# Eight destinations per packed adjacency column, with two-bit counts from destination 256 on

## The chip, the core and the metric

The kernel runs on one core of one Trainium2 chip. The metric is device time in microseconds (us), the median of several runs. TensorE (PE in the profile) multiplies, VectorE (DVE), ScalarE (ACT) and GpSimd (POOL) work on elements, SyncE (SP) issues DMAs.

## The reference

A graph of 6250 nodes and 200000 edges, sorted by destination, goes through two SAGE layers and three message-passing layers. Each of the five needs the sum over all edges into a node of the features of the edge's source:

```python
agg = segment_sum(x[src], dst, num_segments=n)          # SAGE, twice: mean @ W_l.T + b_l + x @ W_r.T
m = concatenate([x[dst_f], x[src_f], ea_f], axis=1) @ W.T + b
agg = segment_sum(m, dst_f, num_segments=n)             # three times, with relu and a batch norm between
```

Destinations are drawn as `6250 * uniform ** 2`, so low node numbers have many edges and high ones few. Sources are uniform.

## The kernel before, in words

The kernel first builds the dense matrix of edge counts (source by destination, as 8-bit floats) and then multiplies node features with it five times.

**The build (function build).** Destinations are cut into windows, and each window into slots of at most 128 edges. There are NS = 1983 slots. For a slot, TensorE multiplies two tables that VectorE makes from the digits of the edges' sources and destinations: `lo` (128 source digits) and `key` (destination lane and source block). One matmul adds the counts of a few *packed columns* to a PSUM bank. A packed column holds four destinations: each has a 4-bit lane of one 16-bit number. A bank holds 8 packed columns of 52 numbers, so 32 destinations, and there are 196 banks, in a ring of RING = 4 PSUM buffers.

The work goes in *half-steps* h of HS = 64 slots (NH = 31 of them), and each engine's order is written out in the code:

- VectorE in half-step h: `large(h)` (one table `lo`, L786, and some pieces of `key`, L793), `attributes(c)` for one chunk c of the edge attributes (L820 to L828), at even h `small` (digit tables for 128 slots, L751 to L770), at odd h `digits` (L736 to L747), then `unpack(f)` for the stages that have become whole. `large(h)` waits until TensorE is through with the slots of half-step h - 2 (`s_pe`).
- ScalarE in half-step h: `high(c)` (L982), `take(f)` (L1017), `evacuate(g)` of the banks that TensorE ended in half-step h - 1 (L998, one bank each, into 16-bit numbers in F), `sums` (L1008), `low(c)` (L988), at even h `across` (L973, L974), which waits for `small`, and `natural` (L959).
- TensorE in half-step h: `product(f)` (L904, 49 matmuls) for the stages that were unpacked after half-step h - 1, then the 64 slots (L929), then chunk c (L942).

A *stage* is 256 destinations, one of NST = 25. `unpack(f)` (L810, L811) takes the packed numbers of the f-th stage apart into 8-bit floats, GpSimd stores them (`keep`), and TensorE multiplies them at once with the first layer's features: `product(f)` for f < 21 (EARLIER), `remaining(f)` (L314) for the last four. All `product`s share one PSUM buffer PX, so the second of two in one half-step waits until ScalarE has taken the first:

```python
def product(f):
    pe.wait_ge(s_un, f + 1)
    if f >= 1:
        pe.wait_ge(s_raw, f)          # take(f - 1) on ScalarE
```

ScalarE does `take(f)` one half-step later in its own order (`for f in multiplied_after(h - 2)`).

`unpack(f)` writes to one of two buffers, so it waits until the stage before the last has been multiplied: `s_px` for `product`, `s_fin` for `remaining`:

```python
v.wait_ge(*((s_px, f - 1) if f - 2 < EARLIER else (m["s_fin"], f - 1 - EARLIER)))
```

**The end of the build.** After the last chunk VectorE makes reciprocals of the early edge counts (`counts`, L1092 to L1098). SyncE then stores them (L587), reads them back over all partitions (`reciprocals`, L299), reads the stored products (L292), the transposed input x (`given`, L305) into F, and the late edge counts (L600). When these are there VectorE does `counts` again and unpacks the last stage, and all engines meet at the end of the block.

**The layers (function propagate).** Five passes of 13 blocks of 512 destinations. In pass 0 the products are already there. In passes 1 to 4 TensorE multiplies 49 x 512 columns per block (L1462). VectorE's `sums` (L1834, L1836) bring the columns, which stand lane by lane in the stored matrix, into their natural order. VectorE's `check` (L1866) adds up the stored matrix in seven rounds, ScalarE's `lanes` (L1995) adds up each lane, and at the end these are compared with the edge counts, so that an overflow of a lane would be seen and a slow general version (`restart`, `general`) run instead.

Of the kernel before, what the change touches and what calls it, by code (L numbers as in the profile page):

```python
# [7 lines left out]
E = 200000  # L8
NT = 49
# [21 lines left out]

def bands(a, b):
# [4 lines left out]
    for j in range(ns):  # L37
        met = [i for i in range(b - a) if most(mu[i + 1]) > 128 * j and mu[i] - Z * math.sqrt(mu[i]) < 128 * (j + 1)]
        if j == 0:
            met.append(0)  # L40
        if j == ns - 1:
            met.append(b - a - 1)
        found.append(((a + min(met)) // 4, (a + max(met)) // 4 - (a + min(met)) // 4 + 1))
# [3 lines left out]
def cut(a, b):  # L47

    best = {b: (0.0, [])}
    for x in range(b - 4, a - 4, -4):  # L50
        options = []
        for y in range(x + 4, b + 1, 4):
            w = bands(x, y)
            if max(q for _, q in w) <= 4:
# [20 lines left out]
BANK = 32  # L75
BANKS = [cut(a, a + BANK) for a in range(0, NP, BANK)]
# [37 lines left out]
SLOT = [(x // 4, j, qa, width, i == 0, i == len(w) - 1)  # L114
# [5 lines left out]
NBK = NP // BANK  # L120
RING = 4
LAST_OF = [max(k for k in range(NS) if SLOT[k][2] // 8 == b) for b in TURN]
BEGUN = {st: min(g for g in range(NBK) if TURN[g] // 8 == st) for st in range(NST)}
DONE = {st: max(g for g in range(NBK) if TURN[g] // 8 == st) for st in range(NST)}
STAGES = sorted(range(NST), key=lambda st: DONE[st])
RANK = {st: f for f, st in enumerate(STAGES)}
HOME, BEFORE = {}, {}
for _st in sorted(range(NST), key=lambda st: BEGUN[st]):
    _users = {h: max((DONE[x] for x in HOME if HOME[x] == h), default=-1) for h in range(4)}
    HOME[_st] = min(_users, key=lambda h: _users[h])  # L130
    assert _users[HOME[_st]] < BEGUN[_st]
    BEFORE[_st] = max((RANK[x] + 1 for x in HOME if HOME[x] == HOME[_st] and x != _st), default=0)
# [103 lines left out]
GIVEN = [(0, 2), (2, NB)]  # L236
# [3 lines left out]
def stage_width(s):  # L240
    return SW if s < NST - 1 else LASTW

# [28 lines left out]
def spread(m, name, cnt, a, b):  # L271

    x = (m["ea_sum"][32, :] if name == "ea_sum" else m[name])[a:b]
    return x.rearrange("(p c) -> p c", p=16), cnt[:, 0:(b - a) // 16]
# [49 lines left out]
def gnn(nc, ins, out):  # L324
    ctx = ExitStack()
    with ctx:
# [3 lines left out]
        def sem(name):  # L330
# [32 lines left out]
            "csum": sb("csum", [16, 2, 4]),  # L363
# [13 lines left out]
def build(nc, ins, m):  # L377
    ctx = ExitStack()
    with ctx:
# [28 lines left out]
        nb = within(0, [128, TS], f32)  # L408
# [41 lines left out]
        packed = m["F"][:].bitcast(u16).rearrange("p (r c) -> p r c", r=4)  # L450
# [92 lines left out]
        def _(sp):  # L543
# [3 lines left out]
            sp.dma_start(nb[:], ins["c_nb"]).then_inc(s_con, 16)  # L547
# [20 lines left out]
            for c in range(NCH):  # L568
# [6 lines left out]
                if c == NCH - 2:  # L575
                    for i in range(2):
                        sp.wait_ge(s_eo[i], 16 * (EARLY // SW // 2))
                    there, here = spread(m, "ea_sum", cnt, 0, EARLY)
                    sp.dma_start(here, there).then_inc(m["s_cl"], 16)
# [11 lines left out]
            sp.wait_ge(m["s_cd"], 16)  # L591
# [11 lines left out]
            sp.wait_ge(m["s_cr"], 8)  # L603
# [3 lines left out]
            given(sp, ins, m, 1)  # L607
# [90 lines left out]
        def _(v):  # L698
# [30 lines left out]
            def digits(t):  # L729
# [9 lines left out]
                op(d[:, 3], node, -4, None, ALU.bitwise_and)  # L739
                op(d[:, 4], node, 4, 0x20, ALU.logical_shift_left, ALU.bitwise_and)  # L740
                op(d[:, 5], node, 6, 0x40, ALU.logical_shift_left, ALU.bitwise_and)
# [57 lines left out]
            def unpack(f):  # L799
# [1380 lines left out]
```

## Time and profile before

| what | value |
|---|---|
| runs of the kernel before | 1074.97, 1079.38, 1078.5 us, median 1078.5 us |
| the profiled execution's own time | 1073.11 us |
| its span, first to last instruction | 1071.3 us |
| busy in the span: PE, DVE, ACT, POOL | 923.9, 686.6, 406.3, 131.8 us |
| mean granted TensorE clock | 0.951 of full speed |
| end of the build, where all engines meet | 405 us after the span's start |

The busy times are those of the whole span, and an engine's share differs much between the build (up to 405 us) and the layers (after it). A time in the trace is counted from the span's start. Where instructions of VectorE follow each other without a wait, each begins a little before the one ahead has ended, so the step from start to start is what one costs.

### The profile page before, as it was taken

The page shows a single profiled execution, that of the slowest core. Times are in us where ns is not written, and L with a number is a line of the kernel's source. Part 1 is how long each engine was busy: PE and PEld are TensorE (multiplying, and loading weights), DVE is VectorE, ACT ScalarE, POOL GpSimd, SP SyncE. Part 2 cuts the span into 40 slices and gives each one's busy share as a digit, 9 for nine tenths or more (in the row PEclk, how much of TensorE's full clock was granted, in tenths as well). Part 3 has the DMA queues.
Part 4 walks back from the last instruction along what each step waited for, and adds up shares of the span by engine and source line. Part 5 has one row for each costly group of instructions (what it writes and reads, how often), then busy time and mean ns, then how long its engine had stood idle before and what let it go on. Part 6 is the DMA issues. An engine that isn't in the chain of part 4 may idle for free. (4 is left out here: it accounts for less than half of the span.)

```text
span 1071.3 us, 19165 instructions
## 1 busy us (share of the span) xinstructions
PE 923.9 (86%) x7566; PEld 566.3 (53%) x7566; DVE 686.6 (64%) x1288; ACT 406.3 (38%) x847; POOL 131.8 (12%) x150
## 2 busy tenths in 40 slices
PE   0357877979788778999999999997999997999995
PEld 0356776878687765545555544444444444444443
DVE  6898989999999954624433756655395456332334
ACT  2684788888888821100000010104411022401113
POOL 4212313244232320000000000000000000000001
PEclk9868989889899998999999999998999998999998
DMA  6735546756665497964774607776018775037771
GB/s 145 182 97 183 190 137 196 254 160 197 197 207 173 125 338 234 364 247 150 306 312 184 251 22 301 305 266 258 16 33 324 290 281 242 10 115 289 270 282 31
DMA packets 65160, 218.63 MB, mean 204 GB/s; under 512 B 28986, under 2 KB 42891, under 8 KB 51523
## 3 DMA queue, kind: packets, MB, share of 16 engines
q1 hardware_dynamic: 55444, 164.26, 43.2%
q0 software_dynamic: 9616, 53.04, 14.5%
q8 instruction: 62, 1.02, 0.4%
q14 instruction: 38, 0.31, 0.1%
HBM read 170.43 MB, written 45.22 MB: 201 GB/s over the span
## 5 line engine op out<-in xcount | busy, mean ns | idle before, releaser
L1462 PE MATMUL PM<-Aring,Xop 128*128 128x512 fp8e4 (+1 forms) x1960 | 396.7, 363 | 2.3 <-issue 2.3
L1462 PEld LDWEIGHTS PM<-Aring,Xop 128*128 128x128 f16 x1960 | 182.3, 98 | 214.1 <-issue 11.3
L1462 PE MATMUL PM<-Ares,Xop 128*128 128x512 fp8e4 x588 | 136.4, 387 | 2.7 <-ACT Xop L2074 1.2
L1836 DVE TENSOR_SCALAR S<-PM 128x256 f32<-128x256 f32 x72 | 30.6, 424 | 153.2 <-PE PM L1462 64.8
L929 PE MATMUL PM<-Aring 128*128 128x104 fp8e4 (+3 forms) x1616 | 95.2, 217 | 35.1 <-ACT F L998 35.0
L2025 ACT ACTIVATE F<-PH,bag 64x512 f32<-64x512 f32 (+1 forms) x39 | 25.7, 659 | 260.8 <-PE PH L1679 260.3
L929 PEld LDWEIGHTS PM<-Aring 128*128 128x128 fp8e4 x1616 | 85.7, 103 | 38.1 <-ACT F L998 36.9
L1462 PEld LDWEIGHTS PM<-Ares,Xop 128*128 128x128 f16 x588 | 56.0, 99 | 70.1 <-issue 7.3
L1592 POOL DMA_DIRECT2D out<-hT x12 | 9.0, 754 | 652.1 <-DVE hT L1793 652.1
L786 DVE TENSOR_TENSOR Aring<-Ares 128x4096 uint16<-128x4096 uint16 x31 | 70.9, 2287 | 4.9 <-PE PW L929 4.6
L998 ACT ACTIVATE F<-PM 128x392 uint16<-128x392 f32 x147 | 66.6, 516 | 6.7 <-PE PM L929 5.4
L1866 DVE TENSOR_TENSOR hT<-hT,Aring 128x1536 uint16<-128x1536 uint16 (+2 forms) x71 | 67.6, 952 | 2.3
L793 DVE TENSOR_TENSOR Aring<-Ares 128x1144 uint16<-128x1144 uint16 (+22 forms) x139 | 67.4, 551 | 0.0
L904 PE MATMUL PX<-Aring,Xop 128*128 128x256 fp8e4 x490 | 57.0, 278 | 6.9 <-ACT Ares L1017 6.9
L904 PE MATMUL PX<-Xop 128*128 128x256 fp8e4 (+1 forms) x539 | 59.5, 272 | 0.6 <-ACT Ares L1017 0.6
L1834 DVE TENSOR_TENSOR S<-PM,rc 128x256 f32<-128x256 f32 (+1 forms) x25 | 9.4, 415 | 76.5 <-PE PM L1462 74.2
L929 PE MATMUL PW<-Aring 128*128 128x104 fp8e4 (+3 forms) x535 | 34.5, 210 | 26.3 <-ACT F L998 24.2
L904 PEld LDWEIGHTS PX<-Aring,Xop 128*128 128x128 f16 x490 | 48.4, 100 | 13.3 <-issue 7.0
L904 PEld LDWEIGHTS PX<-Xop 128*128 128x128 f16 x539 | 51.3, 100 | 7.1 <-issue 0.8
L2017 ACT ACTIVATE st_<-st_ 128x4 f32<-128x4 f32 (+1 forms) x13 | 2.7, 205 | 131.6 <-DVE st_ L1767 131.6
L942 PE MATMUL PA<-Ares,ea 128*128 128x64 f16 (+1 forms) x1000 | 42.0, 208 | 3.5 <-ACT odd L1009 3.5
L882 PE MATMUL PT<-ident,Ares 128*128 128x128 f32 x32 | 8.7, 365 | 39.9 <-ACT Ares L960 39.9
(170 smaller groups left out, 1265.6 us busy)
## 6 DMA issues: line engine op xcount, KB each, us to landing
Aring<-adj SPq DMA_DIRECT2D x72, 1568.0 KB, 9.8
adj<-Aring POOLq DMA_DIRECT2D x12, 1568.0 KB, 7.0
adj<-Xop POOLq DMA_DIRECT2D x12, 1568.0 KB, 6.8
Ares<-adj SPq DMA_DIRECT2D x6, 1568.0 KB, 20.2
rc<-ea_sum SPq DMA_DIRECT2D x36, 128.0 KB, 6.6
Aring<-adj SPq DMA_DIRECT2D x4, 784.0 KB, 4.6
rc<-rc_d SPq DMA_DIRECT2D x12, 256.0 KB, 9.7
eaf<-in_erow SPq DMA_DIRECT2D x60, 51.0 KB, 2.1
```

The source lines that it names most:

```text
L786: nc.vector.tensor_tensor(lo[:, h % 2].rearrange("p s (i j e) -> p s i j e", i=8, e=2), At[:, t % 2, at:at + HS].rearrange("p s i (o e) -> ...
L793: last = nc.vector.tensor_tensor(key[:, o:o + 26 * n].rearrange("p (q v e) -> p q v e", v=26, e=2), Dv[:, t % 2, d, i:i + n].rearrange("p ...
L904: last = nc.tensor.matmul(PX[:, 0:n], m["Xop"][0][:, h, :], of[:, h, :], start=h == 0, stop=h == NT - 1)
L929: last = nc.tensor.matmul(PW[begun % RING][:, c:c + 52 * (z - y)].rearrange("p (d v b) -> p d v b", d=z - y, b=2), lo[:, h % 2, i, :].bitc ...
L942: last = nc.tensor.matmul(PA[st % 2][:, o:o + 2 * PD].rearrange("p (d e) -> p d e", e=2)[:, :, e:f], ea_flat[:, c % 2, j * GW:j * GW + 128 ...
L998: nc.scalar.activation(to, PW[g % RING][:, 0:416].rearrange("p (q h) -> p h q", h=52)[:, 0:NT], ACT.Copy, scale=32.0).then_inc(s_wev, 1)
L1462: last = nc.tensor.matmul(o, x[:, h, :], rhs, start=h == 0, stop=h == NT - 1)
L1592: g.dma_start(out[b * 512:(b + 1) * 512, :].rearrange("(j q) f -> q j f", q=128), fin[:, b % 4]).then_inc(s_o[b % 4], 16)
L1834: last = nc.vector.tensor_tensor(part, of, natural(by), ALU.mult)
L1836: own(nc.vector.tensor_single_scalar(part, of, 1 / CS, ALU.mult))
L1866: own(nc.vector.tensor_tensor(to[:, 0:h1 - h0], to[:, 0:h1 - h0], of[:, h0:h1], ALU.add))
L2025: nc.scalar.activation(F[0:64, c:c + w], PH[b // 2 % 2][64 * (b % 2):64 * (b % 2) + 64, 0:w], ACT.Relu, bias=t["bag"][:, 4 + conv:5 + conv ...
```

## The change

From destination 256 on, a packed column holds eight destinations with two bits each. The first stage keeps four destinations with four bits.

- A bank from destination 256 on covers 64 destinations. There are 102 banks for 196, with the same shape, and NS = 1840 slots in NH = 29 half-steps. Slots are at most three packed columns wide (four before), so `key` has three destination tables. The elements of all `key` pieces fall from 105820 in 139 instructions to 85124 in 114.
- A packed stage takes half the room: five homes of half the size at the end of F, where there were four. `unpack` takes four instructions of 1568 numbers for two of 3136.
- The first 2048 columns of x now have room in F beside the homes, and are read in the middle of the build (`given(0)`). The next 1536 columns are `given(1)`, behind the reciprocals and the second piece of products, ahead of the late counts.
- The 30 chunks of attributes go into 28 half-steps: half-steps 14 and 28, the last, have two each.
- Edge counts are compared in eight classes. `lanes` has eight instructions of 416 elements per round for four of 832, and `sums` reads PSUM straight and writes every fourth element.
- The stages become whole at other half-steps, so the order of `unpack` and `product` against the rest moves.

```diff
-BANK = 32
-BANKS = [cut(a, a + BANK) for a in range(0, NP, BANK)]
+BANKS = [cut(a, a + 32) for a in range(0, SW, 32)] + [cut(a, a + 64) for a in range(SW, NP, 64)]
...
+NHOME = 5
...
-GIVEN = [(0, 2), (2, NB)]
+GIVEN = [(0, 4), (4, 7), (7, NB)]
...
+                if c == NCH // 2:
+                    given(sp, ins, m, 0)
...
-            sp.wait_ge(m["s_cr"], 4)
-            there, here = spread(m, "rc_d", cnt, 0, EARLY)
-            sp.dma_start(there, here).then_inc(m["s_cd"], 16)
+            sp.wait_ge(m["s_cr"], 6)
+            for there, here in early_parts(m, "rc_d", cnt):
+                sp.dma_start(there, here).then_inc(m["s_cd"], 16)
...
-            sp.wait_ge(s_un, 1 + max(RANK[st] for st in range(NST) if HOME[st] == 0))
-            given(sp, ins, m, 0)
             reciprocals(sp, m, 1)
             products(sp, m, 1)
+            sp.wait_ge(s_un, 1 + max(RANK[st] for st in range(NST) if HOME[st][0] < 2))
+            given(sp, ins, m, 1)
...
-                of = packed[:, HOME[st], 0:NT * n // 4].rearrange("p (h a q) -> p a h q", h=NT, a=2)
-                to = stage[f % 2][:, 0:NT * n // 2].rearrange("p (h z a q) -> p z a h q", h=NT, z=2, a=2)
-                nc.vector.tensor_scalar(to[:, 0], of, 0x0F0F, None, ALU.bitwise_and)
-                nc.vector.tensor_scalar(to[:, 1], of, 4, 0x0F0F, ALU.logical_shift_right,
-                                        ALU.bitwise_and).then_inc(s_un, 1)
+                z, mask = (2, 0x0F0F) if st == 0 else (4, 0x0303)
+                to = stage[f % 2][:, 0:NT * n // 2].rearrange("p (h z q) -> p z h q", h=NT, z=z)
+                nc.vector.tensor_scalar(to[:, 0], packed(st), mask, None, ALU.bitwise_and)
+                for i in range(1, z):
+                    last = nc.vector.tensor_scalar(to[:, i], packed(st), 8 // z * i, mask, ALU.logical_shift_right,
+                                                   ALU.bitwise_and)
+                last.then_inc(s_un, 1)
...
-        def by_quad(x):
-
-            return x.rearrange("p (z q e) -> p q z e", z=2, e=2)
-
-        def natural(x):
-            return x.rearrange("p (q z e) -> p q z e", z=2, e=2)
+        def by_lane(x, z):
+
+            return x.rearrange("p (z m) -> p z m", z=z)
+
+        def natural(x, z):
+            return x.rearrange("p (m z) -> p z m", z=z)
...
-        for i in range(4):
-            x = t["acc"].rearrange("p (h z q) -> p h z q", h=13, z=2)[:, :, i // 2, :].bitcast(u8)
+        for i in range(8):
+            x = t["acc"].rearrange("p (h z q) -> p h z q", h=13, z=4)[:, :, i // 2, :].bitcast(u8)
```

The order moves at two places that matter below. The first is TensorE's order in the build. PX is written by `product`, PT by a transpose at the end of an even half-step, PM and PW are the ring of banks, PA takes the attributes. Before, in most half-steps one product stood alone ahead of the slots, as here:

```order
592 L942 MATMUL PA<-Ares,ea 128x64 x5
593 L942 MATMUL PA<-Ares,ea 128x32
594 L942 MATMUL PA<-Ares,ea 128x64 x5
595 L882 MATMUL PT<-ident,Ares 128x128 x2
596 L904 MATMUL PX<-Xop 128x256 x49
597 L929 MATMUL PM<-Aring 128x52 x11
598 L929 MATMUL PW<-Aring 128x52 x8
```

In the changed kernel two products stand together ahead of the slots of half-step 12:

```order
434 L974 MATMUL PM<-Aring 128x104 x2
435 L974 MATMUL PM<-Aring 128x52
436 L987 MATMUL PA<-Ares,ea 128x64 x32
437 L949 MATMUL PX<-Aring,Xop 128x256 x49
438 L949 MATMUL PX<-Xop 128x256 x49
439 L974 MATMUL PM<-Aring 128x104 x4
440 L974 MATMUL PM<-Aring 128x52 x4
```

Such pairs stood at half-steps 4 and 7 before. They now stand at 4, 12, 20 and 23.

The second place is VectorE's order at the end of the build, after the last `large`. Ares<-eaf and eaf<-eaf,ea are a chunk of attributes, csum<-Ares begins `counts`, R<-R,b begins work that only the layers need. Before:

```order
590 L820 TENSOR_TENSOR Ares<-eaf,Ares 128x12
591 L823 TENSOR_TENSOR Ares<-Ares 128x2048
592 L828 TENSOR_TENSOR eaf<-eaf,ea 128x12x16
593 L1092 TENSOR_REDUCE csum<-Ares 16x4
594 L1094 TENSOR_SCALAR Ares<-Ares 16x224
595 L1096 RECIPROCAL Ares<-Ares 16x224
596 L1098 TENSOR_SCALAR Ares<-Ares 16x224
597 L862 TENSOR_TENSOR R<-R,b 128x3136
```

In the changed kernel:

```order
544 L858 TENSOR_TENSOR Ares<-eaf,Ares 128x12
545 L861 TENSOR_TENSOR Ares<-Ares 128x2048
546 L866 TENSOR_TENSOR eaf<-eaf,ea 128x12x16
547 L846 TENSOR_SCALAR Xop<-F 128x49x32
548 L848 TENSOR_SCALAR Xop<-F 128x49x32 x3
549 L846 TENSOR_SCALAR Aring<-F 128x49x32
550 L848 TENSOR_SCALAR Aring<-F 128x49x32 x3
551 L899 TENSOR_REDUCE csum<-Ares 16x2x2 x2
552 L1139 TENSOR_REDUCE csum<-Ares 16x8
553 L1147 TENSOR_SCALAR Ares<-Ares 16x224
554 L1149 RECIPROCAL Ares<-Ares 16x224
555 L1151 TENSOR_SCALAR Ares<-Ares 16x224
```

`unpack(22)` and `unpack(23)` now stand between the last chunk and `counts`. Before, `unpack(22)` stood a half-step earlier and `unpack(23)` behind the work on R.

## Rows read from the trace of the kernel before

**Rows 1.** Busy time of each engine in three stretches.

```profile
core 0: us, PE busy (x) PEld busy (x) DVE busy (x) ACT busy (x) POOL busy (x), PEclk, DMA share, GB/s
180.00:376.00 196.00, 160.91 (x2520) 149.67 (x2519) 194.84 (x314) 165.86 (x318) 64.17 (x78) 0.93 0.62 190
376.00:405.00 29.00, 19.07 (x210) 17.02 (x207) 14.78 (x22) 5.09 (x15) 7.08 (x8) 0.90 0.81 300
405.00:1071.00 666.00, 639.98 (x3207) 302.83 (x3207) 322.31 (x662) 115.74 (x301) 9.65 (x14) 0.98 0.57 216
```

**Rows 2.** What DVE waited for up to 400 us: in total, times, longest.

```profile
DVE eaf L828 <- ACT ea L982: 7.2, 2, 4.5
DVE Aring L786 <- PE PW L929: 4.6, 2, 4.4
...
DVE Aring L810 <- ACT F L998: 2.4, 2, 1.6
```

**Rows 3.** DVE's two costliest groups up to 480 us: busy, mean ns | idle before.

```profile
L786 DVE TENSOR_TENSOR Aring<-Ares 128x4096 uint16<-128x4096 uint16 x31 | 70.9, 2287 | 4.9 <-PE PW L929 4.6 <-ACT Ares L974 0.3
L793 DVE TENSOR_TENSOR Aring<-Ares 128x1144 uint16<-128x1144 uint16 (+22 forms) x139 | 67.4, 551 | 0.0
```

**Rows 4.** DVE's timeline, 20 to 92 us: start, length, instruction [idle before].

```profile
68.92 0.56 DVE L810 TENSOR_SCALAR Xop<-F 128x1568 uint16<-128x1568 uint16 x1
69.39 0.56 DVE L811 TENSOR_SCALAR Xop<-F 128x1568 uint16<-128x1568 uint16 x1
...
79.16 1.55 DVE L751 TENSOR_TENSOR Ares<-Ares 128x1024 uint16<-128x1024 int16 x3
...
83.53 0.98 DVE L810 TENSOR_SCALAR Xop<-F 128x3136 uint16<-128x3136 uint16 x1
84.42 0.97 DVE L811 TENSOR_SCALAR Xop<-F 128x3136 uint16<-128x3136 uint16 x1
```

**Rows 5.** DVE's timeline, 90 to 165 us: digits, and its waits there.

```profile
92.64 0.19 DVE L736 TENSOR_SCALAR Ares<-Ares 128x128 int16<-128x128 int16 x1
...
98.61 2.29 DVE L786 TENSOR_TENSOR Aring<-Ares 128x4096 uint16<-128x4096 uint16 x1 [4.42 <-PE PW L929]
...
134.17 0.98 DVE L810 TENSOR_SCALAR Aring<-F 128x3136 uint16<-128x3136 uint16 x1 [1.55 <-ACT F L998]
...
152.66 1.23 DVE L828 TENSOR_TENSOR eaf<-eaf,ea 128x1024 f32<-128x1024 f32 x1 [2.68 <-ACT ea L982]
```

**Rows 6.** ACT's and PE's timelines around the first pair of products.

```profile
83.43 1.97 ACT L973 COPY Ares<-Ares 128x2048 uint16<-128x2048 uint16 x1 [3.08 <-DVE Ares L757]
...
88.98 6.90 PE L904 MATMUL PX<-Aring,Xop 128*128 128x256 fp8e4 x49 [6.87 <-ACT Ares L1017]
95.72 1.21 PE L929 MATMUL PM<-Aring 128*128 128x156 fp8e4 x16
```

**Rows 7.** Timeline of all engines at the end of the build.

```profile
376.95 0.53 DVE L1092 TENSOR_REDUCE csum<-Ares 16x4 f32<-16x224 f32 x1
379.78 5.51 PE L314 MATMUL PM<-Aring,Xop 128*128 128x256 fp8e4 x49
380.45 0.33 SPq L587 DMA_DIRECT2D rc_d<-Ares  x1
...
384.66 0.32 SPq L299 DMA_DIRECT2D Aring<-rc_d  x1
...
399.80 0.43 DVE L1092 TENSOR_REDUCE csum<-Ares 16x4 f32<-16x168 f32 x1 [12.50 <-DMA Ares<-ea_sum]
...
405.00 0.71 PEld L1442 LDWEIGHTS PB<-scl,wc 33*64 33x64 f32 x6 [9.29 <-issue]
```

**Rows 8.** ACT groups: evacuations up to 480 us, lanes after 440 us.

```profile
L998 ACT ACTIVATE F<-PM 128x392 uint16<-128x392 f32 x147 | 66.6, 516 | 6.7 <-PE PM L929 5.4 <-PE PW L929 1.0
...
L1995 ACT ACTIVATE junk<-hT 128x832 uint8<-128x832 uint8 x28 | 25.0, 894 | 4.3 <-PEq L1169 3.6
```

**Rows 9.** DVE groups by form: a stepped read, and sums out of PSUM.

```profile
L1092 DVE TENSOR_REDUCE csum<-Ares 16x4 f32<-16x224 f32 x1 | 0.5, 525 | 0.0
...
L1836 DVE TENSOR_SCALAR S<-PM 128x256 f32<-128x256 f32 x72 | 30.6, 424 | 153.2 <-PE PM L1462 64.8 <-issue 39.5 <-PE PH L1679 35.5
```

More of the change, by code:

```diff
@@ L49, in cut @@
     best = {b: (0.0, [])}
-    for x in range(b - 4, a - 4, -4):
+    u = 4 if b <= SW else 8
+    for x in range(b - u, a - u, -u):
         options = []
-        for y in range(x + 4, b + 1, 4):
+        for y in range(x + u, b + 1, u):
             w = bands(x, y)
-            if max(q for _, q in w) <= 4:
+            if max(q for _, q in w) <= (4 if u == 4 else 3):
                 options.append((sum(150 + 26 * q for _, q in w) + best[y][0], [(x, y, w)] + best[y][1]))
@@ L119, with stage_of, place_of @@
 NH = -(-NS // HS)
-NBK = NP // BANK
+NBK = len(BANKS)
 RING = 4
 LAST_OF = [max(k for k in range(NS) if SLOT[k][2] // 8 == b) for b in TURN]
-BEGUN = {st: min(g for g in range(NBK) if TURN[g] // 8 == st) for st in range(NST)}
-DONE = {st: max(g for g in range(NBK) if TURN[g] // 8 == st) for st in range(NST)}
+def stage_of(bank):
+    return 0 if bank < 8 else 1 + (bank - 8) // 4
+def place_of(bank):
+    return bank if bank < 8 else (bank - 8) % 4
+BEGUN = {st: min(g for g in range(NBK) if stage_of(TURN[g]) == st) for st in range(NST)}
+DONE = {st: max(g for g in range(NBK) if stage_of(TURN[g]) == st) for st in range(NST)}
 STAGES = sorted(range(NST), key=lambda st: DONE[st])
 RANK = {st: f for f, st in enumerate(STAGES)}
+NHOME = 5
 HOME, BEFORE = {}, {}
 for _st in sorted(range(NST), key=lambda st: BEGUN[st]):
[L129 to L132, printed above, removed]
+    _users = {h: max((DONE[x] for x in HOME if h in HOME[x]), default=-1) for h in range(NHOME)}
+    HOME[_st] = [NHOME - 2, NHOME - 1] if _st == 0 else [min(_users, key=lambda h: _users[h])]
+    assert all(_users[h] < BEGUN[_st] for h in HOME[_st])
+    BEFORE[_st] = max((RANK[x] + 1 for x in HOME if x != _st and set(HOME[x]) & set(HOME[_st])), default=0)
 def pairs(n):
@@ L407, in build @@
         off = within(0, [128, TS], f32)
-        nb = within(0, [128, TS], f32)
+        nb = within(0, [128, 2, TS], f32)
         io = within(0, [128, 46, 16], i16)
@@ L606, in _ @@
             sp.wait_ge(s_un, NST)
[L607 removed]
+            given(sp, ins, m, 2)
         @block.gpsimd
@@ L858, in _ @@
                 if h == NH - 1:
-                    v.wait_ge(m["s_cl"], 16)
-                    counts(nc, v, cnt[:], m["csum"][:, 0, :], m["s_cr"], 0)
+                    v.wait_ge(m["s_cl"], 48)
+                    for i in range(2):
+                        nc.vector.tensor_reduce(
+                            m["csum"][:, 0, :].rearrange("p (z f e) -> p f z e", z=2, f=2)[:, i],
+                            cnt[:, 8 * i:8 * i + 8].rearrange("p (q e z) -> p z e q", e=2, z=2), AX.X,
+                            ALU.add).then_inc(m["s_cr"], 1)
+                    classes(nc, cnt[:, SW // 16:EARLY // 16], m["csum"][:, 1, :], m["s_cr"])
+                    counts(nc, v, cnt[:], m["s_cr"], 3)
             v.wait_ge(s_w, 16 * 15)
@@ L869, in _ @@
                 unpack(f)
-            v.wait_ge(m["s_cl"], 32)
-            counts(nc, v, late, m["csum"][:, 1, :], m["s_cr"], 4)
+            v.wait_ge(m["s_cl"], 64)
+            classes(nc, late, m["csum"][:, 2, :], m["s_cr"])
+            counts(nc, v, late, m["s_cr"], 7)
             unpack(NST - 1)
@@ L958, in natural @@
                     act.wait_ge(s_tp, t - 1)
-                nc.scalar.activation(nat[:, t % 2, 0, :], rows[:, t % 3, :, 0], ACT.Identity, bias=nb[:, t:t + 1])
+                nc.scalar.activation(nat[:, t % 2, 0, :], rows[:, t % 3, :, 0], ACT.Identity, bias=nb[:, 0, t:t + 1],
+                                     scale=nb[:, 1, t:t + 1])
                 nc.scalar.copy(nat[:, t % 2, 1, :], rows[:, t % 3, :, 1]).then_inc(s_nat, 1)
@@ L1062, in _ @@
             for h in range(NH + 1):
-                if h < NH:
-                    for c in CHUNKS[h]:
-                        high(c)
+                chunks = CHUNKS[h] if h < NH else []
+                before = [c for c in chunks if c - 2 not in CHUNKS[h - 1]]
+                for c in before:
+                    high(c)
                 for f in multiplied_after(h - 2) if h >= 2 else []:
@@ L1072, in _ @@
                     sums(st)
-                for c in CHUNKS[h] if h < NH else []:
+                for c in chunks:
+                    if c not in before:
+                        high(c)
                     low(c)
```

129 lines of the change are left out of this document (73 added, 56 removed).

## The prediction, made before the changed kernel ran

> **What bounds the kernel now.** I read the busy times by stretch first [rows 1]. From 180 to 376 us DVE is busy 194.8 of 196 us, PE 160.9 and ACT 165.9: this part of the build runs at DVE's pace. From 376 to 405 us DVE is busy 14.8 of 29 us, so this stretch is a chain. After 405 us PE is busy 640 of 666 us: the layers are PE's, and the change leaves PE's work there as it is. The waits of DVE [rows 2] show what is left for other engines in the build: 14.2 us, in six waits. Three of the four long ones stand behind a pair of products [rows 5]: 4.4 us at 94 us, and 1.6 and 2.7 us at 134 and 152 us. The fourth, 4.5 us, comes at the start, while ACT casts x, and I leave it as it is. So a gain must come out of DVE's instructions, and it counts only if the order of the half-steps and the chain to 405 us let it through. That ACT loses 94 evacuations of 0.516 us [rows 8], 48 us in all, and PE 229 matmuls of slots, is worth nothing by itself: in DVE's stretch both had time to spare.
>
> **What DVE saves.** Two of 31 `large` tables go: 70.9 / 31 = 2.29 us each [rows 3], 4.6 us. The pieces of `key` are busy 67.4 us [rows 3]. Scaled by elements (85124 / 105820) they save 13.2 us, by instructions (114 / 139) 12.1; I take 13, since most of the pieces are long. One `small` goes: from 79.16 to 83.53 us [rows 4], 4.4 us. In ten others the destination table is a quarter shorter, about 0.1 us each by estimate, 1 us. One `digits` goes: from 92.64 us to the wait that begins at 98.61 - 4.42 = 94.19 us [rows 5], 1.6 us. Against this, `unpack`: an instruction of 3136 numbers costs 84.42 - 83.53 = 0.89 us and one of 1568 costs 69.39 - 68.92 = 0.47 us [rows 4], so a stage costs 4 x 0.47 = 1.88 us for 1.78. On 24 stages that is 2.4 us. By full lengths (4 x 0.56 for 2 x 0.98) it would be 6.7 us, which is the upper bound. Together 4.6 + 13 + 4.4 + 1 + 1.6 - 2.4 = 22.2 us. `unpack(22)`, 1.8 us, also moves behind the last chunk, so the last chunk of attributes on DVE ends 24 us earlier, at some 353 us, if no wait is added.
>
> **What the pairs of products take.** At 83.43 us ACT begins `across`, which had waited for DVE's `small`. Only after that, `natural` and `high` come `take`, and PE has sat idle 6.87 us when its second product starts at 88.98 us. It takes 6.90 us, and the slots begin at 95.72 us [rows 6]. DVE's next `large` but one waits for these slots: 4.4 us [rows 5]. The second pair was behind an odd half-step, without `across`, and cost 1.6 + 2.7 = 4.3 us [rows 5]. The changed order has four pairs for two. The one at half-step 12 is followed by an `unpack` that needs a bank in the middle of that half-step, and the one at 20 has `across` behind it as the first had. So I charge two more pairs at 4.3 us: +8.6 us. The bounds are 0 (ACT has three or four banks to empty in a half-step, where it had six or seven, and PE's ring never fills) and twice that. In half-step 14 DVE's second chunk waits for ACT's `low` and `high`: +1 us.
>
> **What the end of the build takes.** Set t0 at the end of the last chunk, 376.95 us before [rows 7]. There `counts` began at once and the store of the reciprocals (L587) went out at 380.45, t0 + 3.5. In the changed order `unpack(22)` and `unpack(23)` come first. `unpack(23)` waits for `remaining(21)`, and that stands behind all of PE's slots and the last evacuations. Before, this product began at 379.78, t0 + 2.8, and took 5.5 us [rows 7]. So `unpack(23)` starts at t0 + 8.3 and ends at t0 + 10.2, and everything on SP that is queued behind the early reciprocals comes 10.2 us later: L587, the reciprocals over all partitions, the second piece of products, x and the late counts. Two more stores and two more small sums make it 10.7. Then comes the transfer that ended last: from the first read of reciprocals at 384.66 to the late counts at 399.80 us, 15.1 us [rows 7], in which the DMA engines also carried `unpack(23)`'s store. In the changed order this store goes ahead of the reads, but x's piece is half as large again. I take 2 us off for it (0 to 5 are possible). The end, from 399.8 to 405.0 us, is the same. The charge is +8.7 us, with 4 to 11 as bounds.
>
> **What the layers take.** `lanes` was 0.894 us for 832 elements [rows 8], four times a round; eight of half the size carry the same elements and four fixed costs more, some 1.5 us a round by estimate, in seven rounds, on an engine that is busy 116 of 666 us [rows 1]. I charge 1 us of 10, for rounds in which DVE's next `check` is waiting. `sums` writes every fourth element, see below. Sum: -22.2 - 1.8 + 8.6 + 1 + 8.7 + 1 = -4.7 us.
>
> **The rivals.** (1) The pairs cost nothing, because ACT has less to do around them: -4.7 - 8.6 = -13.3 us, 1065 us. For it: ACT was the one named in two of the three waits. Against it: in the first, ACT itself was waiting for DVE [rows 6], and that stays. (2) The end of the build is not later: -13.4 us, 1065 us. It needs `remaining(21)` to be ready before DVE asks, and the order forbids that; or the DMA stretch shrinks by all of the 8.7 us. Both together would give 1056 us. (3) Slower: PE falls from its upper to its lower clock level (1.2 GHz) while it is idle ahead of a pair's second product. The first second product took 6.90 us where others take 5.51 [rows 6, 7]; at half the clock throughout it would take 11, and the slots behind it (95.72 to about 98.3 us) 2.6 us more. That is 6.7 us more for each of the two new pairs, 13.4 us, and 1087 us; it decides once it brings over 10 us. Against it: the one such product in the trace took only a fourth more. (4) The stepped writes of `sums` cost. A read in steps of four f32 numbers took 525 ns for 224 elements, where 256 elements out of PSUM took 424 [rows 9], so about 0.15 to 0.3 us more for each instruction of `sums`. In pass 0 (26 of them, about 3 us of PE's chain per block) that could be 4 to 8 us if nothing hid it; later it is hidden behind a block's matmuls except at the end of a pass. With +5 us: 1079 us. Beside this, the Trainium skill ("SBUF — State Buffer", section "Door 1: The DMA port swizzle") says that SBUF has 16-byte lines, that each access to a new line pays, and that PSUM wants contiguous access. By that rule the change trades a friendlier PSUM read for a write that meets a new line with each element, as (4) has it. (5) The change doesn't do what it says, because a two-bit lane overflows and the slow version runs. In the reference's inputs no pair of source and destination from 256 on has more than three edges: under 1 in 100.
>
> **How the numbers follow.** The sum is made against the profiled execution's 1073.1 us, which lies 5.4 us under the median of the runs shown, 1078.5. By the sum the profiled execution would be 1068.4 and the median 1078.5 - 4.7 = 1074 us. 0.5% is 5.4 us, about what a measurement of this kernel can tell from no change. The forecast gets 0.50, with a range of its own from 1068 to 1080 (savings off by 2, pairs by 4, the end by 3): 0.18 of it below 1073.1, 0.32 within 0.5%. (1) gets 0.13, (2) 0.10 and both 0.02, all faster. (3) gets 0.10, slower. (4) gets 0.13, within. 0.02 are left over, within. So faster 0.43, same 0.47, slower 0.10. The range from 1063 to 1082 takes in (1), (2) and (4) and leaves out most of (3) and both together.
>
> **What would show it.** DVE's busy time up to the last chunk should be 24 us less, with 54 us for `key`. Its waits in the build should be about 23 us for 14, with new ones of 4 us or more behind half-steps 12 and 20. At the last chunk DVE should wait some 6 us for `remaining(21)` ahead of `unpack(23)`, and the time from the end of the last chunk to the meeting of the engines should be 36 to 37 us for 28. From there to the end it should be 666 to 668 us. I am wrong if the waits behind the pairs are absent, if the early counts start at once after the last chunk, or if the layers differ by over 3 us.

## The result, and the profile of the changed kernel

| | before | changed |
|---|---|---|
| median of the runs | 1077.61 us (1074.97 to 1079.38) | 1121.48 us (1120.47 to 1124.67) |
| profiled execution, its span | 1071.3 us | 1120.3 us |
| mean granted TensorE clock | 0.951 | 0.920 |

The ratio is 1.0414, with a 95% interval of 1.0383 to 1.0446. The forecast was 1074 us, within 1063 to 1082. So the change costs 44 us where I had forecast no measurable change.

I divide the span at two moments of the trace: t0, where VectorE's first instruction behind the last chunk of attributes begins, and the meeting of the engines, where PE begins L1442 (L1495 in the changed kernel). Up to t0 the profile gives DVE's busy time, and the rest is its idle time. First the stretch up to t0 of the changed kernel (columns as in [rows 1]):

```profile
core 0: us, PE busy (x) PEld busy (x) DVE busy (x) ACT busy (x) POOL busy (x), PEclk, DMA share, GB/s
0.00:406.88 406.88, 257.02 (x3951) 233.21 (x3952) 361.98 (x603) 241.73 (x424) 97.78 (x126) 0.85 0.55 164
```

| us | before | changed | difference | forecast |
|---|---|---|---|---|
| DVE busy up to t0 | 350.5 | 362.0 | +11.5 | -24.0 |
| DVE idle up to t0 | 26.5 | 44.9 | +18.4 | +9.6 |
| t0 to the meeting | 28.1 | 42.4 | +14.3 | +8.7 |
| the layers | 666.3 | 671.0 | +4.7 | +1 |
| span | 1071.3 | 1120.3 | +49.0 | -4.7 |

The largest error is in DVE's work, which should have fallen by 24 us and rose by 11.5. Its groups by form up to 470 us (busy, mean ns of one | idle before, what ended it; the last row is of all forms together) say where:

```profile
L848 DVE TENSOR_SCALAR Xop<-F 128x1568 uint16<-128x1568 uint16 x36 | 32.5, 958 | 0.0
L848 DVE TENSOR_SCALAR Aring<-F 128x1568 uint16<-128x1568 uint16 x33 | 29.8, 959 | 0.0
L846 DVE TENSOR_SCALAR Aring<-F 128x3136 uint16<-128x3136 uint16 x1 | 1.8, 1779 | 0.0
L822 DVE TENSOR_TENSOR Aring<-Ares 128x4096 uint16<-128x4096 uint16 x29 | 66.2, 2284 | 4.8 <-PE PM L974 4.5 <-ACT Ares L1020 0.3
...
L829 DVE TENSOR_TENSOR Aring<-Ares 128x988 uint16<-128x988 uint16 (+17 forms) x114 | 54.6, 541 | 0.0
```

`large` (L822) and `key` (L829) fell as forecast, to 66.2 and 54.6 us. But `unpack` (L846, L848) pays 959 ns for 1568 numbers, where the row I had taken my price from showed 560 [rows 4]. In stage 0, which has the same elements as before, an instruction of 3136 numbers takes 1779 ns, where it was 980. The elements are those of before; the time of one has gone up by 1.7 to 1.8 times.

What DVE waited for up to 420 us (in total, times, longest; before in [rows 2]):

```profile
DVE Aring L846 <- ACT F L1042: 12.2, 3, 6.9
DVE eaf L866 <- ACT ea L1028: 10.3, 5, 6.1
DVE Aring L846 <- PE PM L341: 7.3, 1, 7.3
DVE Aring L822 <- PE PM L974: 4.5, 1, 4.5
...
DVE Ares L858 <- DMA eaf<-in_erow: 3.3, 1, 3.3
```

The waits that the prediction had counted (14.2 us before, some 23 forecast) are 30.3 us in these lines, without the one for L341. The one of 6.1 us for ACT's `high` (L1028) stands at 48 us, at the start, where the kernel before waited 4.5. The other long ones of the half-steps stand behind three of the four pairs of products, in DVE's timeline (start, length, [idle before]):

```profile
102.18 0.97 DVE L846 TENSOR_SCALAR Aring<-F 128x1568 uint16<-128x1568 uint16 x1 [4.70 <-ACT F L1042]
...
205.28 0.97 DVE L846 TENSOR_SCALAR Aring<-F 128x1568 uint16<-128x1568 uint16 x1 [6.95 <-ACT F L1042]
...
321.23 2.29 DVE L822 TENSOR_TENSOR Aring<-Ares 128x4096 uint16<-128x4096 uint16 x1 [4.54 <-PE PM L974]
```

And the end of the build, which answers to [rows 7], in the timeline of all engines:

```profile
406.88 0.96 DVE L846 TENSOR_SCALAR Xop<-F 128x1568 uint16<-128x1568 uint16 x1
...
410.43 7.18 PE L341 MATMUL PM<-Aring,Xop 128*128 128x256 fp8e4 x49
...
417.75 0.97 DVE L846 TENSOR_SCALAR Aring<-F 128x1568 uint16<-128x1568 uint16 x1 [7.27 <-PE PM L341]
...
421.40 0.50 DVE L1139 TENSOR_REDUCE csum<-Ares 16x8 f32<-16x208 f32 x1
...
424.97 1.69 SPq L623 DMA_DIRECT2D rc_d<-Ares  x3
...
442.31 0.44 DVE L1139 TENSOR_REDUCE csum<-Ares 16x8 f32<-16x168 f32 x1 [12.63 <-DMA Ares<-ea_sum]
...
449.28 0.77 PE L1495 MATMUL PB<-scl,wc 33*64 33x1 f32 x6 [20.97 <-PEq L406]
```

`unpack(23)` waits 7.3 us for `remaining(21)`, and only at t0 + 14.4 do the early counts begin, which before began at t0.

### The profile page after: what moved, and what is told of

It reads as the page before. It is cut to its first block and busy times, and to the rows that moved or that the text cites. A ratio compares the mean times of both kernels' runs of the same rounds, so it can differ in the third digit from the quotient of the medians.

```text
span 1120.3 us, 18654 instructions
## 1 busy us (share of the span) xinstructions
PE 918.8 (82%) x7335; PEld 553.0 (49%) x7335; DVE 727.9 (65%) x1296; ACT 371.2 (33%) x797; POOL 115.5 (10%) x148
## 5 line engine op out<-in xcount | busy, mean ns | idle before, releaser
L1515 PEld LDWEIGHTS PM<-Aring,Xop 128*128 128x128 f16 x1960 | 182.4, 98 | 217.2 <-issue 15.2
L1890 DVE TENSOR_SCALAR S<-PM 128x256 f32<-128x256 f32 x72 | 43.5, 604 | 141.6 <-PE PM L1515 62.5
L974 PE MATMUL PM<-Aring 128*128 128x52 fp8e4 (+2 forms) x1468 | 74.7, 212 | 31.5 <-ACT F L1042 29.5
L974 PEld LDWEIGHTS PM<-Aring 128*128 128x128 fp8e4 x1468 | 70.5, 103 | 33.2 <-ACT F L1042 30.5
L949 PE MATMUL PX<-Aring,Xop 128*128 128x256 fp8e4 x490 | 62.7, 294 | 25.2 <-ACT Ares L1061 25.2
L949 PE MATMUL PX<-Xop 128*128 128x256 fp8e4 (+1 forms) x539 | 65.8, 288 | 13.3 <-ACT Ares L1061 13.3
L822 DVE TENSOR_TENSOR Aring<-Ares 128x4096 uint16<-128x4096 uint16 x29 | 66.2, 2284 | 4.8 <-PE PM L974 4.5
L949 PEld LDWEIGHTS PX<-Aring,Xop 128*128 128x128 f16 x490 | 51.0, 105 | 34.8 <-issue 25.6
L1888 DVE TENSOR_TENSOR S<-PM,rc 128x256 f32<-128x256 f32 (+1 forms) x25 | 13.9, 604 | 72.4 <-PE PM L1515 70.1
L829 DVE TENSOR_TENSOR Aring<-Ares 128x988 uint16<-128x988 uint16 (+17 forms) x114 | 54.6, 541 | 0.0
L987 PEld LDWEIGHTS PA<-Ares,ea 128*128 128x128 f16 x1000 | 38.2, 107 | 19.7 <-ACT odd L1053 16.3
L1034 ACT ACTIVATE ea<-eaf 128x1024 f16<-128x1024 f32 (+1 forms) x30 | 31.1, 1038 | 42.9 <-DVE eaf L866 42.7
```

The source lines that it names most:

```text
L822: nc.vector.tensor_tensor(lo[:, h % 2].rearrange("p s (i j e) -> p s i j e", i=8, e=2), At[:, t % 2, at:at + HS].rearrange("p s i (o e) -> ...
L829: last = nc.vector.tensor_tensor(key[:, o:o + 26 * n].rearrange("p (q v e) -> p q v e", v=26, e=2), Dv[:, t % 2, d, i:i + n].rearrange("p ...
L949: last = nc.tensor.matmul(PX[:, 0:n], m["Xop"][0][:, h, :], of[:, h, :], start=h == 0, stop=h == NT - 1)
L974: last = nc.tensor.matmul(PW[begun % RING][:, c:c + 52 * (z - y)].rearrange("p (d v b) -> p d v b", d=z - y, b=2), lo[:, h % 2, i, :].bitc ...
L987: last = nc.tensor.matmul(PA[st % 2][:, o:o + 2 * PD].rearrange("p (d e) -> p d e", e=2)[:, :, e:f], ea_flat[:, c % 2, j * GW:j * GW + 128 ...
L1034: nc.scalar.mul(part(c % 2, n, 16), eaf[:, c % RE, 0:n, 0:16].rearrange("p (g s) c -> p g s c", s=2), LO).then_inc(s_lo, 1)
```

## The experiments

Lengths up to t0 come from each kernel's profiled execution, totals are medians, and ratios are to the kernel before on the same chip (1075.9, 1075.0 and 1075.6 us in the three groups of runs, experiments 1 to 4, 5 to 8, and 9 and 10).

**1. The shape of `unpack` alone.** The elements and the four instructions stay. Only the innermost 32 is written as 2 x 16 with the two outermost among the dimensions, as before:

```diff
-                to = stage[f % 2][:, 0:NT * n // 2].rearrange("p (h z q) -> p z h q", h=NT, z=z)
-                nc.vector.tensor_scalar(to[:, 0], packed(st), mask, None, ALU.bitwise_and)
+                of = packed(st).rearrange("p h (a q) -> p a h q", a=2)
+                to = stage[f % 2][:, 0:NT * n // 2].rearrange("p (h z a q) -> p z a h q", h=NT, z=z, a=2)
+                nc.vector.tensor_scalar(to[:, 0], of, mask, None, ALU.bitwise_and)
```

> The changed kernel, with unpack's four instructions written with a dimension of two outermost (128 x 2 x 49 x 16), as the kernel before had them; same elements, masks and shifts. Theory A (the shape of the access, not its length, made an instruction of 1568 numbers cost 0.88 us): it costs 0.47 us from start to start, as the row of stage 24 before had it; a stage costs 1.9 us for 3.5, some 40 us over 25 stages, and the time is about 1081 us for 1121.5. Theory B (the fixed cost of four instructions for two, the two-bit mask and shift, or the place of the homes in F): the instruction keeps 0.88 us and the time stays at 1121 us. Theory C (a shorter inner run of 16 numbers costs more): between, or above 1121 us.

Measured: 1099.23 us (1096.76 to 1102.33), ratio 1.0211 [1.0180, 1.0242]. By form:

```profile
L849 DVE TENSOR_SCALAR Xop<-F 128x1568 uint16<-128x1568 uint16 x36 | 18.1, 558 | 0.0
L849 DVE TENSOR_SCALAR Aring<-F 128x1568 uint16<-128x1568 uint16 x33 | 16.7, 561 | 0.0
L847 DVE TENSOR_SCALAR Aring<-F 128x3136 uint16<-128x3136 uint16 x1 | 1.0, 970 | 0.0
```

The price of the instruction is settled: it hangs on the shape alone. But the total fell by 22 us, not by 40. The stretch up to t0 shows why:

```profile
0.00:392.31 392.31, 252.95 (x3937) 229.76 (x3938) 327.85 (x604) 241.87 (x424) 117.88 (x126) 0.85 0.55 170
```

DVE's work fell by 34.1 us to 327.9, which is 22.6 us less than before the change, close to the forecast of 24. Its idle time rose from 44.9 to 64.5 us. So the slow `unpack` had covered waits, and there was a second error in the forecast. The timeline of all engines around the pair at half-step 12:

```profile
168.26 6.28 PE L950 MATMUL PX<-Aring,Xop 128*128 128x256 fp8e4 x49
...
175.35 1.96 ACT L1020 COPY Ares<-Ares 128x2048 uint16<-128x2048 uint16 x1 [3.08 <-DVE Ares L793]
...
181.24 8.26 PE L950 MATMUL PX<-Xop 128*128 128x256 fp8e4 x49 [6.70 <-ACT Ares L1062]
...
191.61 0.57 DVE L847 TENSOR_SCALAR Aring<-F 128x1568 uint16<-128x1568 uint16 x1 [8.15 <-ACT F L1043]
...
192.78 1.05 ACT L1035 ACTIVATE ea<-eaf 128x1024 f16<-128x1024 f32 x1
...
193.99 5.06 SPq L620 DMA_DIRECT2D eaf<-in_erow  x8
...
208.14 0.26 DVE L859 TENSOR_TENSOR Ares<-eaf,Ares 128x64 int16<-128x64 int32 x1 [7.83 <-DMA eaf<-in_erow]
```

The second product waits 6.7 us for `take`, which stands behind `across` and so behind DVE's `small`, and then takes 8.3 us. The banks come late, and `unpack` waits 8.15 us for the last. ACT's `low` (192.78) stands behind these evacuations, and the load of a later chunk needs the buffer that `low` frees. It is issued at 193.99 and has landed 14 us later, at 208.14, and DVE waits another 7.83 us for it, ahead of the second chunk of half-step 14. The two waits make 16 us, and the second of them stands elsewhere and under another name.

**2. The same shape in the kernel before.** Its two instructions per stage without the dimension of two:

```diff
-...rearrange("p (h a q) -> p a h q", h=NT, a=2)
-                to = stage[f % 2][:, 0:NT * n // 2].rearrange("p (h z a q) -> p z a h q", h=NT, z=2, a=2)
+...rearrange("p (h q) -> p h q", h=NT)
+                to = stage[f % 2][:, 0:NT * n // 2].rearrange("p (h z q) -> p z h q", h=NT, z=2)
```

> The kernel before, with only the dimension of two taken out of unpack's two instructions (128 x 49 x 64 for 128 x 2 x 49 x 32). Theory A: each costs about 1.7 us from start to start for 0.89, 1.6 us a stage, and the time goes from 1077.6 to about 1117 us. Theory B: nothing changes, 1078 us.

Measured: 1102.60 us (1099.73 to 1105.07), ratio 1.0241 [1.0213, 1.0270].

```profile
L810 DVE TENSOR_SCALAR Aring<-F 128x3136 uint16<-128x3136 uint16 x12 | 21.4, 1780 | 4.0 <-ACT F L998 2.9 <-PE PM L314 1.0
...
L811 DVE TENSOR_SCALAR Xop<-F 128x3136 uint16<-128x3136 uint16 x12 | 21.3, 1774 | 0.0
```

In the kernel before these took 972 ns. DVE's busy time up to t0 rose by 36.5 us and t0 moved by 34.8, from 376.95 to 411.76. The meeting moved by 32 us only, since DVE's wait for the late counts shrank from 12.5 to 6.7 us. The shape alone slows the kernel by 2.4%, without anything else of the change; less than the 39 us that I had expected, and much more than nothing.

**3. The early counts first.** Experiment 1 with `unpack(22)` and `unpack(23)` behind the early counts:

```diff
-                for f in unpacked_after(h):
+                for f in unpacked_after(h) if h < NH - 1 else []:
                     unpack(f)
...
                     counts(nc, v, cnt[:], m["s_cr"], 3)
+            for f in unpacked_after(NH - 1):
+                unpack(f)
```

> e1_unpack_pairs, and the early counts stand ahead of unpack(22) and unpack(23) after the last chunk on VectorE. If the wait of unpack(23) for remaining(21) delays all that is queued on SyncE behind the early reciprocals, as the prediction had it (10 us, 8.7 after the shorter transfer), the meeting of the engines comes some 8 us sooner against e1_unpack_pairs and the time is about 1073 us. Rival: the stretch is set by the late counts alone, whose chain starts with the last edge sums; then nothing, 1081 us.

Measured: 1090.48 us (1084.33 to 1099.04), ratio 1.0140 [1.0073, 1.0206]. The runs scatter by 15 us, so the difference to experiment 1, 8.8 us, is rough. The traces are clearer: from t0 to the meeting it is 31.4 us for 37.4. So some 6 us of the 9.3 by which the end had grown belong to this order, and DVE's wait for the late counts is down from 12.5 to 7.3 us. Experiment 4, which has the build of experiment 1, took 40.5 us there, so it may be 9 us.

**4. `sums` with whole lines.** Experiment 1 with the step of four on the side that is read, in PSUM, as the kernel before has it:

```diff
-            return x.rearrange("p (z m) -> p z m", z=z)
+            return x.rearrange("p (z m) -> p m z", z=z)
...
-            return x.rearrange("p (m z) -> p z m", z=z)
+            return x.rearrange("p (m z) -> p m z", z=z)
```

> e1_unpack_pairs, and sums writes its columns one after the other and reads PSUM (and the sums of pass 0) in steps, instead of the other way round. Theory D (the stepped write makes an instruction of sums 604 ns for 424): back to about 424 ns, and the layers lose the 4.7 us that they took more than before: 1076 us. Theory E (a step on either side costs the same): 604 ns and 1081 us.

Measured: 1098.81 us (1095.52 to 1102.56), ratio 1.0215 [1.0177, 1.0252]. By form, in the layers of the changed kernel, and then of this one (from 460 to 1062 us only, so 68 of the 72):

```profile
L1890 DVE TENSOR_SCALAR S<-PM 128x256 f32<-128x256 f32 x72 | 43.5, 604 | 141.6 <-PE PM L1515 62.5 <-issue 33.7 <-PE PH L1732 32.2
```

```profile
L1891 DVE TENSOR_SCALAR S<-PM 128x256 f32<-128x256 f32 x68 | 28.8, 424 | 139.2 <-PE PM L1516 61.5 <-issue 36.6 <-PE PH L1733 28.5
```

The write in steps costs 180 ns an instruction, as rival (4) had it, and with the read in steps out of PSUM instead it is 424 ns, as in [rows 9]. The 20 instructions of pass 0 that read SBUF hardly gained: 616 ns in the changed kernel, 586 here, 422 before. Yet the layers took 669.0 us for 670.8. The idle column shows why: DVE waits for PE's matmuls before nearly all of these. The gain that I had expected in the total did not come.

**5. The products of a pair in half-steps of their own.** Experiment 3, and each product at least one half-step behind the one ahead (TensorE and ScalarE both use this list, so `take` moves too):

```diff
+        at = []
+        for f in range(EARLIER):
+            at.append(max(stage_end[f] + 1, at[-1] + 1 if at else 0))
+
         def multiplied_after(h):
 
-            return [f for f in unpacked_after(h) if f < EARLIER]
+            return [f for f in range(EARLIER) if at[f] == h]
```

> e3_counts_first, and no two products stand in one half-step: of a pair the second goes one half-step later (and those behind it where needed). In e3_counts_first and e1_unpack_pairs VectorE waits 4 to 8 us behind each of the four pairs, 23 to 24 us in all. Theory F (the pair is the cause, since the second product waits for ScalarE's take a half-step later and TensorE's slots stand behind it): these waits fall to under 6 us and the time goes from 1090 to some 1070 us. Rival (ScalarE or TensorE is simply late there, and the waits move to the next unpack): within 5 us of 1090 us.

Measured: 1069.80 us (1068.70 to 1070.75), ratio 0.9955 [0.9938, 0.9971], so 20.7 us less than experiment 3.

```profile
0.00:364.57 364.57, 251.19 (x3951) 228.01 (x3952) 327.64 (x603) 241.93 (x424) 116.22 (x126) 0.88 0.60 183
```

DVE's work is that of experiments 1 and 3 (327.6 for 327.9 and 328.1 us) and its idle time 36.9 for 64.5 and 63.2. All products together kept PE busy for 127.3 us here and 128.8 in experiment 1, so it isn't their length that costs here, but that two stand in a row.

**6. The second chunk of half-step 14 at the half-step's end**, on DVE and ACT, on top of experiment 5:

```diff
-                for c in CHUNKS[h]:
+                chunks = list(CHUNKS[h])
+                later = chunks[1:] if h < NH - 1 else []
+                for c in chunks[0:len(chunks) - len(later)]:
                     attributes(c)
...
                     unpack(f)
+                for c in later:
+                    attributes(c)
```

> e5_products_apart, and in half-step 14, which has two chunks of attributes, the second one stands at the end of the half-step instead of behind the first. In e1_unpack_pairs VectorE waited 7.8 us there for the chunk's data, whose load can only be issued after the chunk two before. If that load is the cause, the wait goes and the time falls by 5 to 8 us against e5_products_apart; if SyncE's issue of the loads is the limit in any order, the wait moves to chunk 15 and nothing changes.

Measured: 1067.23 us (1066.20 to 1069.13), ratio 0.9928 [0.9909, 0.9946]: 2.6 us less, half of the low end of what was expected. DVE's waits around half-step 14 fell from 6.8 to 3.9 us, but t0 came 0.5 us later in the trace, since DVE was idle for 3.0 us more in the first 60 us, where both kernels have the same order.

**7. Experiment 6 with the edit of experiment 4.**

> e6_second_chunk_late, with the sums of e4_sums_whole_lines, 424 ns for 604 out of PSUM. By e4_sums_whole_lines (1098.8 for 1099.2) this is worth 0 to 2 us. If all theories hold, this version is the fastest, near 1062 us, under the kernel before (1076).

Measured: 1066.44 us (1064.47 to 1067.81), ratio 0.9914 [0.9895, 0.9934]. The 0.8 us to experiment 6 lie within the scatter, which fits that the stepped write is hidden.

**8. The kernel before with only the edit of experiment 5.**

> The kernel before, with only its two pairs of products taken apart as in e5_products_apart. Theory F: VectorE's waits of 4.4, 1.6 and 2.7 us go, and the time falls by 4 to 9 us, 1067 to 1072 for 1076. Rival: the waits of the kernel before were of the ring of banks, not of the pairs; then 1076 us.

Measured: 1066.33 us (1064.22 to 1068.82), ratio 0.9913 [0.9896, 0.9929]. Without its two pairs the kernel before is 8.6 us faster. It ties with experiment 7, the changed kernel after these repairs, though DVE has 22.4 us more work up to t0 (350.1 for 327.7).

**9. The changed kernel's own `unpack`, without the pairs.** Experiment 5 without the edit of experiment 1:

> The changed kernel with its own unpack (a contiguous shape, some 960 ns for an instruction of 1568 numbers), but with the early counts ahead of the last two unpacks and with the two products of each pair in half-steps of their own. Against the run of the same kernel with the dimension of two outermost in unpack (1069.8 us) it has only the slower instructions: (959 - 560) ns x 4 on 23 stages and (1779 - 970) ns x 2 on stage 0, 38 us of VectorE. Theory A (the waits behind the pairs are what had hidden part of the price, so without them it shows nearly in full): 1069.8 + 33 to 38 = 1103 to 1108 us. Rival H (the price is absorbed by something other than the pairs, half of it, as between the changed kernel and the first experiment, where 22 us of 39 showed): 1069.8 + 22 = 1092 us. Rival I (the pairs cost their 20 us on their own in the changed kernel, in addition to unpack): the same as theory A within 3 us in total, but VectorE then has no more waits than 5 us in the build.

Measured: 1097.83 us (1094.33 to 1099.53), ratio 1.0218 [1.0183, 1.0254], 28.0 us over experiment 5. Neither number was met.

```profile
0.00:390.05 390.05, 254.74 (x3965) 231.69 (x3966) 362.23 (x603) 240.52 (x424) 99.58 (x126) 0.86 0.56 171
```

Against experiment 5 DVE's work is 34.6 us longer and its idle time 9.1 us shorter (27.8 for 36.9). So even with single products a part of the slow instruction goes into waits that were there. With the pairs it was 19.6 us of 34.1.

**10. The first pair together again**, on top of experiment 7:

```diff
-            at.append(max(stage_end[f] + 1, at[-1] + 1 if at else 0))
+            at.append(max(stage_end[f] + 1, at[-1] + 1 if f > 1 else 0))
```

> The fastest of the changed kernel's versions so far (1066.4 us) with the first two products again in one half-step, the later pairs still apart. In that version VectorE waited 3.5 and 6.2 us for products at 94 and 126 us. Theory J (those two waits come from the shift of the first products by a half-step, which makes each unpack meet the product before last): they go, one wait of 4 to 6 us behind the first pair comes back (as in the kernel before, 4.4 us), so 4 to 6 us less in the build, 1061 to 1063 us. Rival K (the first pair costs what the later ones do, some 5 us, and the two waits were due to TensorE's low clock there): no gain, 1066 to 1069 us.

Measured: 1064.54 us (1061.22 to 1065.56), ratio 0.9899 [0.9869, 0.9930], between the two theories. What went and what came, in experiment 7 and then here:

```profile
97.62 0.57 DVE L851 TENSOR_SCALAR Aring<-F 128x1568 uint16<-128x1568 uint16 x1 [3.53 <-PE PX L960]
...
126.19 0.57 DVE L851 TENSOR_SCALAR Aring<-F 128x1568 uint16<-128x1568 uint16 x1 [6.21 <-PE PX L960]
```

```profile
99.76 0.57 DVE L851 TENSOR_SCALAR Aring<-F 128x1568 uint16<-128x1568 uint16 x1 [6.47 <-ACT F L1053]
```

The two waits of 9.7 us went, as theory J said, but the one that came back is 6.5 us. Net 3.3 us are to be had, t0 came 1.2 us earlier, and the median is 1.9 us lower, which the intervals do not separate. It is the fastest version that I ran, 1.0% under the kernel before. Whether experiment 8, which has the old packing, would gain from the same edit wasn't run, so of the packing itself no gain over it is shown.

## Why the prediction was wrong

DVE's busy and idle time up to t0, and what follows, in one table (us; from the profiled executions):

| kernel | busy | idle | t0 | t0 to meeting | layers |
|---|---|---|---|---|---|
| before | 350.5 | 26.5 | 376.95 | 28.1 | 666.3 |
| changed | 362.0 | 44.9 | 406.88 | 42.4 | 671.0 |
| 1, shape | 327.9 | 64.5 | 392.31 | 37.4 | 670.8 |
| 3, and counts first | 328.1 | 63.2 | 391.36 | 31.4 | 667.7 |
| 5, and products apart | 327.6 | 36.9 | 364.57 | 31.2 | 671.2 |
| 9, as 5 with the slow shape | 362.2 | 27.8 | 390.05 | 34.2 | 670.1 |
| 10, the fastest | 327.7 | 35.6 | 363.25 | 31.5 | 668.8 |
| 8, before with products apart | 350.1 | 21.7 | 371.76 | 28.3 | 667.0 |

**The price of `unpack` is the step that failed first.** I took 0.47 us for 1568 numbers from stage 24 [rows 4] and called 6.7 us for all stages the upper bound. That row has the right number of elements and the wrong shape: the code of before has a dimension of two outermost (`a=2` in the diff), the order of the change says 128x49x32, and I compared only the product. Experiments 1 and 2 show both directions: 561 against 959 ns, 972 against 1777 ns. The true price up to t0 is 34 us of DVE's work over experiment 1, and 39 us over all stages. The bound was no bound, since both its ends came from rows of the one shape. In the total the price is worth 22 us of the 47 us between forecast and result, since the slow `unpack` filled waits.

The Trainium skill ("VectorE: DVE Perf Modes", section "What auto-detection actually checks") states a rule that I had passed over: an instruction with 16-bit numbers in steps of one gets its fastest mode only with a single source, both sides in SBUF, and outermost dimensions that are both even or equal. The flat shape writes 49 separate rows and reads one run of 1568 numbers that touch. If the chip takes that run as one, the outermost dimensions are 1568 and 49, one even and one odd, and the rule denies the mode; with two outermost on both sides it grants it. The trace agrees in direction, 1.7 and 1.8 times the time. Which mode was in use, and whether touching rows are taken as one, no row here shows.

**The savings were right.** Without the shape, DVE's work falls by 22.6 us (experiment 1) where I had 24.0 with the moved `unpack(22)`. `large` and `key` came out at the forecast numbers.

**The pairs were right as a mechanism and too small.** I charged 8.6 us for two more, 4.3 each, with 17.2 as the upper bound. Taking four pairs apart gives 20.7 us in the total (3 to 5) and 26.3 in idle time, taking apart the two of before gives 8.6 and 4.8. The difference is what the two new pairs cost: 12 us by the medians, inside my bounds, and 21.5 us by the idle time of the traces, above them. Neither figure is sharp. The medians of experiment 3 lie among runs 15 us apart, and a trace is one execution. Counted from 60 us on, which leaves out the start, DVE is idle for 49.9, 46.9 and 42.6 us in experiments 1, 3 and 4, which all have the four pairs, for 22.2 in experiment 5, 11.6 before and 6.8 in experiment 8. That gives 15 to 23 us for the two new pairs. Each of these figures is above the 8.6 us charged; whether the cost is above 17.2 is open. Two things were missing: the second product takes 7 to 8.3 us where the row had 6.9, and the pair's delay comes back once more when a load of attributes is late (7.8 us at 208 us and 4.5 at 385 us in experiment 1, neither in experiment 5), because ACT's `low` stands behind the delayed evacuations. In the changed kernel itself the slow `unpack` covered a part of this. Rival (3), the low clock, is seen too: the granted clock up to t0 is 0.85 in the changed kernel for 0.90 before, and products of 5.5 us took 7 to 8. In experiment 5 all of them together were as long, and the 20.7 us went all the same.

**The saving is not the gain.** Without any pairs, the changed kernel still has 15.2 us more idle time on DVE than the kernel before without its pairs (36.9 for 21.7), so of 22.4 us less work 7.2 arrive at t0. This was no term of my sum, apart from 1 us for half-step 14, where experiment 1 had 7.8 us of waits and experiment 5 still 3.6 (2.2 and 1.4). I had called PE and ACT engines with time to spare in DVE's stretch; by their shares that is so, but DVE waits for single pieces of their work. Most of the 15.2 us are two waits of `unpack` for a product, 3.5 us at 94 us and 6.2 at 123 us. In experiment 5 and then in experiment 8 (in total, times, longest):

```profile
DVE Aring L851 <- PE PX L956: 9.8, 2, 6.2
```

```profile
DVE Xop L814 <- PE PX L908: 0.4, 1, 0.4
```

The products of experiment 5 keep PE busy for 127.3 us at a granted clock of 0.88 up to t0, those of experiment 8 for 115.9 us at 0.92. How much of the 9.8 us comes from these longer products and how much from the order is open: experiment 10 changed the order and traded 9.7 us for 6.5. By the medians experiments 6 and 10 gained 2.6 and 1.9 us, but DVE's whole idle time hardly moved in the traces (36.9 to 37.3, and 36.7 to 35.6). A third buffer for the loads, which would test a part of the rest, wasn't tried.

**The end of the build went by its own steps.** In experiment 1, with the price of `unpack` that I had assumed, it took 37.4 us for the 36 to 37 forecast (40.5 in experiment 4 with the same build). `unpack(23)` waited 7.2 us for `remaining(21)`, as foreseen (I had 6.4). In the changed kernel the slow shape brings it to 42.4.

**The layers took 4.7 us more, I had 1.** Nine traces of changed kernels lie at 667.7 to 671.2 us, three of kernels with the old layout at 666.1 to 667.0. So some 3 us are real. The traces say where: from the start of the third to the start of the fourth of the passes that multiply, it takes 160.7 to 163.1 us in the nine and 158.6 to 159.7 in the three. Up to the first of these passes there is no such difference (43.3 to 44.8 us for 43.7 to 44.8 after the meeting), so pass 0, where rival (4) saw the stepped write at its dearest, isn't the place, though the 20 of its instructions that read SBUF cost more with both layouts of `sums`. For the later passes experiments 4, 7 and 10 speak against the stepped write as the main part (669.0, 670.2 and 668.8 us with whole lines). Whether `lanes` or the transfers bring the 3 us is open.

Of what I said would prove me wrong, layers that differ by over 3 us did occur, in the changed kernel's trace; the waits behind the pairs and the late early counts came as described.

## What to carry to other kernels

A price is read from a row of the same shape, not of the same number of elements. When an access pattern is rewritten, compare its dimensions one by one, outermost first, and if the trace has no such row, the bound upward is a factor, not a few per cent. A wait that is charged at one place can come back later through a buffer that is freed late, so follow the late engine's queue to the next load. And before a change is built to take work from the bounding engine, try the free reordering first: here it was worth 8.6 us in four lines of code, about as much as the whole change after its repairs (8.5 to 11 us), which include it.

## What the runs showed of the hardware that I had not expected

- VectorE, 16-bit numbers from SBUF to SBUF, 49 rows of 32 or 64: 959 and 1777 ns for 1568 and 3136 elements; the same elements with a dimension of two outermost 561 and 972 ns.
- VectorE from PSUM to SBUF, 256 f32 numbers: 604 ns when it writes in steps of four. Written contiguously and read in steps of 64 it is 424 ns, and instructions of this size that read PSUM without steps took 425 ns. Read in steps out of SBUF, in pass 0 of experiment 4, it is 586 ns.
- GpSimd's instructions are shorter where DVE runs `unpack` at the slow shape. Up to t0 GpSimd is busy for 97.8 us in the changed kernel and 117.9 in experiment 1 (126 instructions each), for 99.6 us in experiment 9 and 116.2 in experiment 5, and for 108.4 us in experiment 2 and 115.9 before. In the first of these comparisons most of the difference lies in 17 indirect loads, up to 360 us: 1086 ns each for 1897. No run shows the cause, and spans on GpSimd are rough.
